# A Mamba-style mixer's output projection as three float32r products, with the residual stream in DRAM

## The reference, cut to what matters

```python
x = x + mixer(layernorm(x), ...)       # state-space mixer, 128 heads of 64
x = x + ffn(layernorm(x), ...)         # 16 experts of 56, top 2
x = x + attention(layernorm(x), ...)   # 32 heads of 16, causal
x = x + ffn(layernorm(x), ...)
```

```python
g = y * silu(gate)                     # (1024 tokens, 8192 channels)
gg = g.reshape(b, s, 8, 1024)
gg = gg * rsqrt(mean(gg * gg, -1, keepdims=True) + 1e-5)
out = gg.reshape(b, s, 8192) * norm_w
return einsum('bsi,oi->bso', out, out_proj_w)      # 8192 -> 512
```

## Time and profile before

| | |
|---|---|
| median of 3 runs | 2751.22 us (2750.11 to 2752.27) |
| profiled execution | 2748.32 us, of which span 2746.5 us |
| PE busy | 2537.2 us, 92% of the span |
| DVE / ACT / POOL busy | 1924.8 / 1452.7 / 392.4 us |
| first and last out-projection | 203.43 us, 1870.75 us |
| out-projections (L617) | 1024 records for 512 products: two each |
| granted TensorE clock, mean | 0.967 of full |

### The profile page before, as it was taken

The page is one execution under the profiler, slowest core; times in us unless marked ns, Lnnn a source line. Parts: engine busy times, 40 slices in busy tenths (PEclk is TensorE's granted clock), DMA queues, the critical chain, the costliest instruction groups (busy, mean ns, idle before and its releaser), DMA issues. The chain is left out here.

```text
span 2746.5 us, 42314 instructions
## 1 busy us (share of the span) xinstructions
PE 2537.2 (92%) x14144; PEld 1770.3 (64%) x14144; DVE 1924.8 (70%) x3759; ACT 1452.7 (53%) x3497; POOL 392.4 (14%) x448
## 2 busy tenths in 40 slices
PE   3579999999999999999999999996989889999799
PEld 2467777777776777776777677764874534444488
DVE  5367878777787787787877887865556467676354
ACT  2265656556657566566666565643223346666311
POOL 2101111111111111110110110122220011111121
PEclk7799999999999999999999999998999989999899
DMA  2322232223223223223323223212013111110000
GB/s 91 97 59 65 66 90 67 62 69 89 64 61 97 63 68 90 59 71 88 67 65 88 67 64 84 68 26 88 0 74 124 66 47 41 36 40 25 1 12 19
DMA packets 195003, 172.68 MB, mean 63 GB/s; under 512 B 31264, under 2 KB 157296, under 8 KB 193136
## 3 DMA queue, kind: packets, MB, share of 16 engines
q1 hardware_dynamic: 189344, 168.13, 22.3%
q10 hardware_dynamic: 5456, 2.00, 0.3%
HBM read 151.70 MB, written 18.38 MB: 62 GB/s over the span
## 5 line engine op out<-in xcount | busy, mean ns | idle before, releaser
L487 PE MATMUL bank<-xh,wh 128*128 128x512 f32 x1152 | 467.4, 406 | 49.4 <-DVE wl L838 33.6
L694 ACT ACTIVATE xch<-bank,pk 128x64 f32<-128x64 f32 x1024 | 219.9, 360 | 530.0 <-PE bank L569 528.9
L617 PE MATMUL bank<-wo,yt 128*128 128x512 f32 x1024 | 452.1, 594 | 16.7 <-issue 13.8
L487 PE MATMUL bank<-xl,wh 128*128 128x512 f32 x1152 | 452.3, 393 | 0.0
L487 PE MATMUL bank<-xh,wl 128*128 128x512 f32 x1152 | 452.2, 393 | 0.0
L812 DVE SCALAR_TENSOR_TENSOR cacc<-raw,cwh,cacc 128x512 f32<-128x512 f32 x480 | 360.5, 751 | 44.4 <-ACT cacc L796 32.9
L617 PEld LDWEIGHTS bank<-wo,yt 128*128 128x128 f32 x1024 | 192.9, 190 | 238.1 <-issue 235.3
L487 PEld LDWEIGHTS bank<-xh,wh 128*128 128x128 f32 x1152 | 218.4, 190 | 97.6 <-DVE wl L838 34.4
L487 PEld LDWEIGHTS bank<-xh,wl 128*128 128x128 f32 x1152 | 218.1, 189 | 47.7
L487 PEld LDWEIGHTS bank<-xl,wh 128*128 128x128 f32 x1152 | 218.7, 190 | 40.3
L2043 ACT ACTIVATE at_PT<-bank 128x512 f32<-128x512 f32 (+3 forms) x384 | 167.4, 498 | 118.3 <-PE bank L1958 113.8
(11 more groups left out here) (246 smaller groups left out, 4637.6 us busy)
## 6 DMA issues: line engine op xcount, KB each, us to landing
xn<-w_hs_dram SPq DMA_DIRECT2D x112, 256.0 KB, 2.7
EC<-ecum_scratch SPq DMA_DIRECT2D x112, 256.0 KB, 8.6
xn<-w_gate_dram SPq DMA_DIRECT2D x80, 256.0 KB, 3.0
wo<-w_out_dram SPq DMA_DIRECT2D x8, 2048.0 KB, 9.1
rawx<-w_gate_dram SPq DMA_DIRECT2D x48, 256.0 KB, 3.1
rawx<-w_hs_dram SPq DMA_DIRECT2D x48, 256.0 KB, 2.7
qk_scratch<-at_part SPq DMA_DIRECT2D x48, 256.0 KB
at_qT<-qk_scratch SPq DMA_DIRECT2D x32, 192.0 KB, 2.6
```

What stands on the lines that cost most here:

```text
L487: mm = nc.tensor.matmul(BA[bank][:, :], w[:, s, k, :], x[:, k, tok], start=(k == 0 and m == 0), stop=(k == KC - 1 and m == 2))
L617: mm = nc.tensor.matmul(BA[b][:, :], yt[:, j * P:(j + 1) * P], wo[:, j, :], start=(j == 0), stop=(j == JT - 1))
L694: o = nc.scalar.activation(xch[:, hh * HP:(hh + 1) * HP], BT[1 - u][:, i * HP:(i + 1) * HP], ACT.Copy, scale=pk[:, h, c, O_DT + hh:O_DT + ...
```

## The change

The out-projection becomes three float32r products. `yt` is split into `yh` (ScalarE, rounded to float32r) and `yl = yt - yh` (GpSimd, written over `yt`). `wo * norm_w` is split into `woh` (ScalarE, where `ac_weigh` was) and `wol` (VectorE, written over `wo`). The squares move into the buffer of the gate's tanh, `sg`. Two folds of the squares now follow each other on VectorE. The residual stream moves to DRAM: each slot loads its 128 tokens into `xz`, adds, and stores them; after the mixer `xr` is loaded again, ahead of the next stage's weights.

```diff
+                sp.dma_start(xr[:, 0, :], x_dram[0:P, :]).then_inc(s_xr[0], 16)
+                sp.dma_start(xr[:, 1:, :], x_dram[P:, :].rearrange("(z p) c -> p z c", p=P)).then_inc(s_xr[1], 16)
                 sp.dma_start(wr[:, :, :], A["gate_w"]).then_inc(s_w, 16)
...
-        wo = sb(ctx, "wo", [P, JT, C])
+        wo, wol = shared("wo", [P, JT, C])
+        woh = sb(ctx, "woh", [P, JT, C], F32R)
...
-        sq = sb(ctx, "sq", [P, JT, P])
-        yt = sb(ctx, "yt", [P, GC])
+        yt, yl = shared("yt", [P, GC])
+        yh = sb(ctx, "yh", [P, GC], F32R)
         sg = sb(ctx, "sg", [P, GC])
+        sq = sg[:, :].rearrange("p (j t) -> p j t", j=JT)
+        xz = sb(ctx, "xz", [P, 2, C])
...
-            pe.wait_ge(wo_set, 17 * g + 17)
...
-            dv_gg.wait(pe, n + 1)
+            dv_wo.wait(pe, JT * (g + 1))
+            po_yl.wait(pe, n + 1)
             for j in range(JT):
-                mm = nc.tensor.matmul(BA[b][:, :], yt[:, j * P:(j + 1) * P], wo[:, j, :], start=(j == 0), stop=(j == JT - 1))
+                for m, (y, w) in enumerate(((yh, woh), (yh, wol), (yl, woh))):
+                    mm = nc.tensor.matmul(BA[b][:, :], y[:, j * P:(j + 1) * P], w[:, j, :],
+                                          start=(j == 0 and m == 0), stop=(j == JT - 1 and m == 2))
...
             for j in (2 * i, 2 * i + 1):
-                o = nc.scalar.activation(wo[:, j, :], wo[:, j, :], ACT.Copy, scale=nw[:, 0, j:j + 1])
+                nc.scalar.activation(woh[:, j, :], wo[:, j, :], ACT.Copy, scale=nw[:, 0, j:j + 1]).then_inc(ac_wo.sem, 1)
...
             dv_gg.wait(act, n + 1)
+            nc.scalar.copy(yh[:, :], yt[:, :]).then_inc(ac_yh.sem, 1)
+            if step:
+                dv_sg.wait(act, gates_done(n, 1))
             pe_ss.wait(act, n)
-            nc.scalar.activation(sq[:, :, :], yt[:, :].rearrange("p (j t) -> p j t", j=JT), ACT.Square).then_inc(ac_sq.sem, 1)
+            nc.scalar.activation(sq, yt[:, :].rearrange("p (j t) -> p j t", j=JT), ACT.Square).then_inc(ac_sq.sem, 1)
...
+        def dv_out_low(dve, g, i):
+            for j in (2 * i, 2 * i + 1):
+                ac_wo.wait(dve, JT * g + j + 1)
+                nc.vector.scalar_tensor_tensor(wol[:, j, :], wo[:, j, :], nw[:, 0, j:j + 1], woh[:, j, :],
+                                               ALU.mult, ALU.subtract).then_inc(dv_wo.sem, 1)
...
+            dve.wait_ge(d_xin[n % 2], 16 * (n // 2 + 1))
+            nc.vector.scalar_tensor_tensor(xz[:, n % 2, :], BA[b][:, :], rr[:, 1:2], xz[:, n % 2, :], ALU.mult, ALU.add)\
...
             if not last:
                 po_pre(pool, *nxt)
+            ac_yh.wait(pool, n + 1)
+            ac_sq.wait(pool, n + 1)
+            nc.gpsimd.tensor_tensor(yl[:, :], yt[:, :], yh[:, :], ALU.subtract).then_inc(po_yl.sem, 1)
             dv_r.wait(pool, n + 1)
...
+                def store_x(n):
+                    dv_out.wait(sp, n + 1)
+                    sp.dma_start(x_dram[n % NT * P:(n % NT + 1) * P, :], xz[:, n % 2, :]).then_inc(d_xout[n % 2], 16)
...
+                store_x(8 * G - 1)
+                for i in range(2):
+                    sp.wait_ge(d_xout[i], 16 * 4 * G)
```

More of the change, by code:

```diff
@@ L108, in build @@
         turned = sem(top, "turned")
-        mixer(nc, A, xr, ident, identb, nhalf, stat, mv, rstd, xn, BANK, pack_dram, rows_dram, ecum_dram, skip_dram, sb, sig, sem, turned, debug)
+        mixer(nc, A, x_dram, ident, identb, nhalf, stat, mv, rstd, xn, BANK, pack_dram, rows_dram, ecum_dram, skip_dram, sb, sig, sem, turned, debug)
+        xr = sb(top, "xr", [P, NT, C])
         wgu = sb(top, "wgu", [P, KC, 2, F])
@@ L116, in build @@
         s_w, s_wd = sem(top, "d_ffn"), sem(top, "d_ffn_down")
+        s_xr = [sem(top, f"d_residual{i}") for i in range(2)]
         with nc.Block() as block:
@@ L123, in build @@
         SG = {}
-        FW = (wgu, wd, wr, s_w, s_wd)
+        FW = (wgu, wd, wr, s_w, s_wd, s_xr)
         ffn(nc, A, FW, SG, xr, ident, nhalf, stat, mv, rstd, xn, BANK, sb, sig, sem, "f1")
@@ L145, in _, with mixer @@
                 sp.wait_ge(s, 16)
-def mixer(nc, A, xr, ident, identb, nhalf, stat, mv, rstd, xn, BANK, pack_dram, rows_dram, ecum_dram, skip_dram, sb, sig, sem, turned, debug):
+def mixer(nc, A, x_dram, ident, identb, nhalf, stat, mv, rstd, xn, BANK, pack_dram, rows_dram, ecum_dram, skip_dram, sb, sig, sem, turned, debug):
     with ExitStack() as ctx:
@@ L157, in mixer, with shared @@
         LAST_TILE = STEPS * NTILE
+        def shared(name, shape):
+            with nc.sbuf_tensor(name, shape, F32) as whole:
+                pass
+            return whole, sb(ctx, name + "_lo", shape, F32R)
         xh = sb(ctx, "xh", [P, KC, T], F32R)
@@ L188, in mixer @@
         with ExitStack() as c0:
+            xr = sb(c0, "x0", [P, NT, C])
             xnT = sb(c0, "xnT", [P, KC, T])
@@ L442, in mixer @@
         d_rw, d_ec = sem(ctx, "d_rw"), sem(ctx, "d_ec")
+        d_xin = [sem(ctx, f"d_xin{i}") for i in range(2)]
+        d_xout = [sem(ctx, f"d_xout{i}") for i in range(2)]
         RAW, TAP = 3, TAPS - 1
@@ L678, in ac_gate_tanh @@
             dv_sg.wait(act, m - 1)
+            pe_ss.wait(act, (m - JT) // 2)
             pe_P.wait(act, q + 1)
@@ L734, in weigh @@
                 if z == 0:
-                    ac_weigh(act, g, i)
+                    ac_out_high(act, g, i)
             if not last:
@@ L930, in dv_slot, with low @@
             dv_fold(dve, n, 0)
+            dv_fold(dve, n, 1)
             if not last:
                 dv_masked(dve, *nxt, (1,))
-            dv_fold(dve, n, 1)
+            def low(i):
+                if z == 0:
+                    dv_out_low(dve, g, i)
             def conv(r):
@@ L944, in silu @@
                     dv_silu_tile(dve, step, mine[r])
+            low(0)
             conv(0)
+            low(1)
             conv(1)
             silu(0)
+            low(2)
             if not last:
                 dv_masked(dve, *nxt, (2, 3))
+            low(3)
             conv(2)
@@ L1086, in slot_loads @@
                         next_decay(g, z)
+                    if z > 0:
+                        store_x(8 * g + z - 1)
                     if z == 0 and not end:
@@ L1096, in slot_loads @@
                         next_tile(number(step, "conv", i) + WR)
+                    if 0 < z:
+                        load_x(8 * g + z + 1)
                     if end:
@@ L1127, in prologue @@
                     po_pre(pool, 0, 0)
-                run(pool, po_slot, prologue, (po_cw, po_xd, po_s1, po_r))
+                run(pool, po_slot, prologue, (po_cw, po_xd, po_s1, po_yl, po_r))
             @block.tensor
@@ L1165, in prologue @@
                         ac_exp(act, 0, 0, q)
-                run(act, ac_slot, prologue, (ac_hi, ac_tail, ac_raw, ac_th, ac_xc, ac_mn, ac_ex, ac_tg, ac_sq))
+                run(act, ac_slot, prologue, (ac_hi, ac_tail, ac_raw, ac_th, ac_xc, ac_mn, ac_ex, ac_tg, ac_yh, ac_sq, ac_wo))
             @block.vector
@@ L1185, in prologue @@
                     dv_masked(dve, 0, 0, range(NQ))
-                run(dve, dv_slot, prologue, (dv_lo, dv_cv, dv_act, dv_sm, dv_M, dv_yo, dv_yd, dv_sg, dv_gg, dv_st, dv_out, dv_r, dv_sq))
-    if debug is not None:
-        debug_dump(nc, debug, "x1", xr, sem)
+                run(dve, dv_slot, prologue, (dv_lo, dv_cv, dv_act, dv_sm, dv_M, dv_yo, dv_yd, dv_sg, dv_gg, dv_wo, dv_st, dv_out, dv_r, dv_sq))
 def norm_transpose(eng, kind, S, xr, ident, nhalf, stat, mv, rstd, xn, xnT, banks):
@@ L1231, in ffn @@
 def ffn(nc, A, FW, SG, xr, ident, nhalf, stat, mv, rstd, xn, BANK, sb, sig, sem, tag, out=None):
-    wgu, wd, wr, s_w, s_wd = FW
+    wgu, wd, wr, s_w, s_wd, s_xr = FW
     with ExitStack() as ctx:
@@ L1279, in ffn @@
         s_rev = SG["rev"]
-        s_out = [sem(ctx, f"{tag}_out{i}") for i in range(2)] if out is not None else None
+        s_out = s_xr
         BX, BG, BU, BH, BO = BANK[0], BANK[1:3], BANK[3:5], BANK[5:7], BANK[7]
@@ L1465, in front @@
                 def front(z, r):
+                    if isinstance(z, int) and z < 2:
+                        dve.wait_ge(s_xr[z], 16)
                     nc.vector.bn_stats(stat[:, r, :], tile(z)).then_inc(v_st.sem, 1)
```

36 lines of the change are left out of this document (22 added, 14 removed).

## The result

The changed kernel takes **3005.43 us** in the median of 4 runs (3002.31 to 3006.88); the kernel before, run beside it, 2751.6. The ratio is 1.092 (95% interval 1.090 to 1.094). The forecast was 2982, between 2915 and 3030.

What follows compares the result with a forecast made beforehand. PE was taken to bound the mixer, busy 215.94 of 218.23 us a group. Terms -80 + 194 + 7 + 42 + 60 + 8 = +231 on 2748.32 gave 2979, with 2.9 for the median 2982 us; range 2915 to 3030.

Steps and rivals of the forecast that it cites:

- Products: Out-projection: 24 float32r products at a tile's pace take 5.62 us, not 6.87; 1.25 us a slot, -80 us.
- the products lose this pace: Rival: out-projection products don't run at a tile's pace, so a slot gains nothing; 3062 us, chance 0.03.
- Waits in slots without tiles: PE waits at the out-projection for `yl`, in 17 slots behind a late `xd` on GpSimd; +194 us.
- `yl` beside VectorE: In slots with tiles GpSimd's `yl` holds up VectorE's folds, mostly covered; `z` = 4 is 0.5 us short; +7 us.
- First slots: First slot of each group: PE waits for `wol`, at the end of VectorE's chain, 5.2 us later; +42 us.
- Clock: Behind long PE waits the product runs at the lower clock, 2.5 or 2.0 us each; +60 us, 0 to 85.
- the clock holds: Rival: PE's waits are as long, but no lower clock follows; 2922 us, chance 0.08.
- Residual stream: Behind the mixer: the last store and its wait, and `wgu` landing later behind 2 MB of `xr`; +8 us.
- the case's own range: The main case, chance 0.75, from 2925 to 3010 us: clock term, `yl` time, and first slots without the hold.
- the products decide: Rival: `yl` is ready about when PE arrives, so waits are hidden; about 2707 us, chance 0.05.
- VectorE becomes the bound: Rival: VectorE's thin cover goes, 1 to 2 us in each of 37 slots; 3020 to 3055 us, chance 0.09.

Runs made afterwards that it cites:

- e3: Changed kernel, but the third product reads `yh` in place of `yl`, so PE doesn't wait for `yl`, which GpSimd still makes; 2818.68 us.
- e5: Changed kernel, but VectorE makes `yl`, right ahead of its folds, and GpSimd doesn't; 2859.75 us.
- e2: Changed kernel with `SHARE` as before the change: four convolution tiles in slots `z` = 0 and 4, three in `z` = 1 and 5; 2978.28 us.
- e11: Changed kernel with 38 to 48 extra products, their result overwritten, filling nearly all of PE's wait in first slots and slots without tiles; 2961.06 us.
- e7: Changed kernel with the load of the rest of the residual (1792 KB) issued behind `wgu` and not ahead of it; 3000.22 us.
- e8: Changed kernel with `yl` on VectorE, products by parts, old `SHARE`, residual load behind `wgu`, `yh` made earlier, last `wol` pair ahead of the masks; 2723.13 us.
- e1: Changed kernel, but GpSimd makes `yl` ahead of `xd`, not behind it; 2993.03 us.
- e6: Changed kernel with the 24 products ordered by parts, not by `j`; in first slots `yh` x `wol` last, with a wait for each `wol`; 2890.51 us.
- e9: The kernel of e8, but GpSimd makes `yl`, ahead of `xd`; 2819.77 us.

## Why the prediction was right, and where it was not

The forecast of 2982 lies 23 us below the result, and its mechanism is the measured one, but for the first slots. By its terms:

- **Products**, -80: measured 6.87 - 5.50 = 1.37 us a slot, -88. The tile's pace was a slightly pessimistic price, and the rival that the products lose this pace is ruled out. A float32 product costs 3.75 of a float32r one. The Trainium skill, "FP8 and Floating Point Precision", TensorE Precision Notes, gives four passes for true float32 and no number of passes for the reduced form; with one for that, as the prediction read it, it would have been 1.72 us a slot. The measurement decides.
- **Waits in slots without tiles**, +194: 193.5, and e3 shows that they are causes and not symptoms. `yl` took 2.34 us where 2.4 were assumed.
- **`yl` beside VectorE**, +7: the two folds take 3.2 us beside `yl` for 1.1 alone, as the hold of a whole instruction assumed. The rows agree with the rule cited with the earlier trace rows (the Trainium skill, "SBUF — State Buffer", Who interferes with whom: whoever starts first keeps the shared ports): VectorE's first fold keeps its 684 ns, GpSimd's `yl` grows from 2.34 to 2.90 us, and the second fold waits. In a `z` = 2 slot everything outside the product takes 22.27 us and not 21.83, 0.44 more. With `yl` on VectorE (e5) such a slot is 27.31 us long and not 27.79, so the excess does hang on GpSimd's `yl`. If it is the same in all 37 slots of the term, it was 16 us and not 7 (worked out).
- **First slots**, +42: measured 79.7 - 13.8 = 66. This is the step that failed: it reckoned with four tiles in the first slot. With three, 8 x 2.8 = 22 us of cover are gone; what is left is 44. With four, e2 has 41.9, so the chain itself was priced rightly.
- **Clock**, +60 (0 to 85): e11 gives 44 back. The sum of all products' time above 5.27 us is 54 in the changed kernel. The sum below takes 54; with e11's 44, what is not placed grows by 10. It is less than forecast since the wait in `z` = 3 costs 1.5 and not 2.5 us. The rival "the clock holds" is ruled out.
- **Residual stream**, +8: the tail from the last out-projection grew from 875.75 to 882.9 us, 7. Of the reason given, `wgu`'s delay, e7 could not show that it sets the end.

Measured in this way the terms come to -88 + 193.5 + 16 + 66 + 54 + 7 = 248; the spans differ by 3000.5 - 2746.5 = 254. The last 6 us I have not placed. That the total came so near owes something to luck: the products gave 8 us more than forecast and `yl` beside VectorE cost 9 more, and these cancel. Nor do the three items named for the case's own range, 2925 to 3010, reach its ends: they give 2921 to 3002, and no item stood for the part in which the result lies.

Of the other rivals, "the products decide" comes near with all the edits of e8, `yl` on VectorE and the products by parts among them: 2723, against its 2707. "VectorE becomes the bound" was no more than the 16 us here, but it is what the obvious mend, e1, ran into.

## What to carry to other kernels

Splitting an operand on the way to an in-order engine puts the split on that engine's path: before moving the split to an idle engine, look at what stands ahead of it there, and at what that engine does to its neighbour while it runs. Order the products by parts, so that the late part comes last: 16 products that need only the early parts ran inside the wait, and `z` = 3 and 4 together fell from 58.58 to 55.06 us (e6). A spare engine's time isn't free: the helper that was to relieve VectorE by 1.22 us a slot cost it 1.53 in the mean, and the kernel 146 us (e5) or 97 (e9).

## What the runs showed of the hardware

- The same 128x1024 subtraction into float32r takes 1223 ns on VectorE (e5) and 2.34 us on GpSimd alone. The Trainium skill, "GPSIMD Engine Reference", Engine selection, says about twice as slow for two inputs; the runs agree, with a ratio of 1.9, and add 2.90 us where VectorE runs beside it.
- After 2.27 us of idling in a slot full of products the granted clock was 0.59 over the next 4.2 us (e1), where after 0.60 us at the same place in the changed kernel it was 1.00, and filling the waits nearly to their end kept every out-projection at full pace (e11). I had thought such short waits harmless, as the 1.7 us waits of the earlier trace rows seemed to be.
- A store of 256 KB in the slots lands 9.0 us after its issue in the median (below), where the stores of the earlier trace rows took 2.0. No item of PE's waits in the mixer names these stores or the loads behind them; SyncE stood still for a store 10 times in the changed kernel, 69.5 us in all.

```profile
x_scratch<-xz SPq DMA_DIRECT2D x64, 256.0 KB, 9.0
```
